# Attention context of a fused kernel: turned by VectorE in 32x32 blocks from a second load instead of by TensorE

## Chip, cores, metric

One NeuronCore of a Trainium2 chip. The metric is the device time of one execution in microseconds (us).

## What is computed

Two layers over 16 batches: a cross-attention with a residual, then a recurrent block on its result. The change touches the first layer, and in it the layer norm of the context and what follows from it:

```python
a = _layer_norm(audio_kv, ln_gamma, ln_beta)          # context (16, 375, 512)
Q = (hidden_states @ Wq.T)                            # tokens (16, 112, 512), 16 heads of 32
K = (a @ Wk.T); V = (a @ Wv.T)
scores = einsum('bhtd,bhsd->bhts', Q, K) * scale      # masked, softmax over the 375 keys
out = einsum('bhts,bhsd->bhtd', attn, V)
out = out.transpose(0, 2, 1, 3).reshape(B, Tt, D) @ Wo.T
return hidden_states + tanh(gate) * out
```

## The kernel before

The program is written engine by engine. Each engine has its own function with a fixed order of instructions, and the engines meet only through counted semaphores. Step `n` of the first layer works on three batches at once: it projects keys and values of batch `n` and forms its row-major scores (`scores`, 4 groups of 4 heads), it attends with batch `n-1` (`key_major_scores`, `weigh_values`), and it prepares the context of batch `n+1` (`ln_stats`, the normalised and turned copy, the query).

TensorE contracts over channels, so the context must lie with channels on partitions. Before, VectorE normalises the context with tokens on partitions (`ln_apply`, L430), TensorE turns it with 12 transposes a batch (`transpose_ctx`, L697) into three PSUM banks used in a ring, and ScalarE reads each turned bank twice, applying gamma and beta: once rounded (`aT_hi`, L572), once whole (`whole`, L576). GpSimd subtracts the two for the low part (`aT_lo`, L340). Keys and values are projected in three passes from the high and low parts (L703 to L705).

One region of PSUM, `score_bank`, holds both kinds of scores in turn, and this ties the engines together:

```python
pe.wait_ge(s_masked, count(later(m, 1), HEADS, g * HG))               # key_major_scores: VectorE has masked the scores in it
pe.wait_ge(s_shifted, count(later(b, -1), C * KT, (g + 1) * KT))      # scores: VectorE has read the key-major scores
```

`mask_scores` (L450) masks row-major scores and finds their extremes, `shift_scores` (L467) shifts key-major scores, `scale_attn` (L474) scales the attended values, and `project_out` (L789) waits for it.

All transfers of the first layer are issued by SyncE in one order (`sync`). The row statistics of a batch, turned by `turn_rows` (L782), are written to DRAM and read back spread over the partitions (`spread_rows`). The context mask for the key-major side is `key_mask8`, 125 partitions by 16 batches by 3 bytes (L296). The start loads context 0, the weights, both masks, context 1 and `wo`; VectorE needs the statistics of batch 1 within step 0.

## Time and profile before

| | us |
|---|---|
| median of 3 runs | 1405.7 (1401.32 to 1408.68) |
| profiled execution | 1402.65 |
| its span in the trace | 1400.8 |
| TensorE busy | 1331.3 (95%) |
| VectorE busy | 928.5 (66%) |
| ScalarE busy | 734.7 (52%) |
| GpSimd busy | 489.8 (35%) |

The first layer takes about the first 600 us, the second the rest. Busy time is a sum over a stage; whether an engine waits is read from the idle time before its instructions and from their order in time.

### The profile page before, as it was taken

To read this page: it belongs to the slowest core of one execution; us is meant where nothing else is said; L and a number is where in the kernel's file an instruction comes from. 1 tells how busy PE (TensorE), PEld (TensorE's weight loads), DVE (VectorE), ACT (ScalarE), POOL (GpSimd) and SP (SyncE) were. 2 spreads that over 40 slices of the span, in tenths; PEclk is the share of its full clock that TensorE was granted. 3 is DMA by queue.
4 is the path that set the end of the run, shared out by engine and by line. 5 is a ranking of instruction groups with operands and counts; after the bars stand their busy time and mean duration, and the time that the engine had idled before them with its cause. 6 is when DMAs were issued, how large, how long until landed. Compare 5 with 4: busy or idle time off the path is not lost.

```text
span 1400.8 us, 42823 instructions
## 1 busy us (share of the span) xinstructions
PE 1331.3 (95%) x17120; PEld 937.6 (67%) x17120; DVE 928.5 (66%) x2431; ACT 734.7 (52%) x1772; POOL 489.8 (35%) x550
## 2 busy tenths in 40 slices
PE   6999999999999999897899999999999999999977
PEld 5777777777777777666566666766676667666624
DVE  3555555555555555547677877787888888887862
ACT  4776677767667667632425453445345434444332
POOL 3222111222222222113346445543555345534540
PEclk9999999999999999988999999999999999999979
DMA  7333222222222223113000010001010110010000
GB/s 228 99 106 106 93 75 63 74 73 71 61 76 74 75 69 101 54 57 122 22 21 14 23 28 21 15 22 28 22 27 9 28 27 22 10 26 22 15 14 14
DMA packets 39529, 73.70 MB, mean 53 GB/s; under 512 B 17797, under 2 KB 20485, under 8 KB 37829
## 3 DMA queue, kind: packets, MB, share of 16 engines
q1 hardware_dynamic: 39365, 71.24, 17.2%
q8 instruction: 136, 2.23, 0.7%
q14 instruction: 28, 0.23, 0.1%
HBM read 60.24 MB, written 7.57 MB: 48 GB/s over the span
## 4 chain that ended last, share of the span: by engine, by line
PE 82%; DVE 8%; issue 6%; DMA 2%; ACT 1%; SPq 1%; POOL 0%; DVEq 0%; ACTq 0%; POOLq 0%
PE b_bank L1831 18%; PE b_bank L1837 12%; PE ring_bank L703 7%; PE ring_bank L704 6%; PE ring_bank L705 6%; PE av_bank L789 4%; PE b_bank L1945 4%; PE score_banks L762 4%; DVE probs L450 3%; PE b_bank L1982 3%; PE score_banks L749 3%; PE b_bank L1971 2%; PE b_bank L1885 2%; DVE probsT L467 2%; PE av_bank L775 2%
## 5 line engine op out<-in xcount | busy, mean ns | idle before, releaser
L1126 POOL TENSOR_TENSOR rst<-rp,st 128x448 f32<-128x448 f32 x192 | 209.7, 1115 | 55.9 <-DVE st L1349 53.9
L450 DVE CUSTOM_DVE_ANT_0 probs<-score_banks,unmask 112x375 f32<-112x375 f32 x256 | 124.8, 544 | 93.0 <-issue 93.0
L595 ACT ACTIVATE probs<-probs,least_inv 112x375 f32<-112x375 f32 x256 | 152.4, 606 | 32.5 <-DVE least_inv L450 32.5
L467 DVE SCALAR_TENSOR_TENSOR probsT<-score_banks,least_cols 125x448 f32<-125x448 f32 x192 | 107.9, 617 | 53.9 <-PE score_banks L762 51.7
L610 ACT ACTIVATE probsT<-probsT,key_mask 125x448 f32<-125x448 f32 x192 | 114.5, 661 | 47.4 <-DVE probsT L467 47.2
L1118 POOL TENSOR_TENSOR xm<-mixed,xa 128x448 f32<-128x448 f32 x80 | 88.0, 1102 | 145.3 <-DVE mixed L1278 140.0
L340 POOL TENSOR_TENSOR aT_lo<-whole,aT_hi 128x375 fp32r<-128x375 f32 x64 | 59.0, 921 | 152.3 <-ACT whole L576 150.2
L375 POOL TENSOR_TENSOR ctx_rstd<-ctx_var_eps,a_eps_exp 125x3 f32<-125x3 f32 x16 | 13.8, 865 | 272.6 <-DVE ctx_var_eps L423 272.6
L703 PE MATMUL ring_bank<-aT_hi,wk_lo 128*128 128x376 f32 x256 | 91.2, 356 | 0.2 <-issue 0.2
L1628 ACT COPY key<-b_bank 128x448 f32<-128x448 f32 x16 | 8.5, 533 | 148.4 <-PE b_bank L1831 148.4
L704 PE MATMUL ring_bank<-aT_lo,wk_hi 128*128 128x376 f32 x256 | 85.5, 334 | 0.0
L705 PE MATMUL ring_bank<-aT_hi,wk_hi 128*128 128x376 f32 x256 | 85.4, 334 | 0.0
L1278 DVE SCALAR_TENSOR_TENSOR mixed<-b_bank,vec_sb,sx 128x112 f32<-128x112 f32 x320 | 82.5, 323 | 1.8 <-PE b_bank L1885 1.8
L703 PE MATMUL ring_bank<-wv_hi,aT_lo 128*126 128x512 f32 x192 | 79.3, 413 | 0.4 <-DVE wv_lo L437 0.4
L1328 DVE TENSOR_TENSOR bv<-bv,ktil 128x392 f32<-128x392 f32 (+6 forms) x112 | 76.1, 679 | 3.9
L704 PE MATMUL ring_bank<-wv_lo,aT_hi 128*126 128x512 f32 x192 | 75.8, 395 | 0.0
L705 PE MATMUL ring_bank<-wv_hi,aT_hi 128*126 128x512 f32 x192 | 75.8, 395 | 0.0
L1945 PE MATMUL b_bank<-rst,b_collect 128*32 128x448 f32 x512 | 66.4, 556 | 3.5 <-POOL rst L1126 3.5
L1101 POOL TENSOR_TENSOR ln_rs<-ln_ve,neg_half 112x1 f32<-112x1 f32 x16 | 9.1, 571 | 171.5 <-DVE ln_ve L1245 171.5
L762 PEld LDWEIGHTS score_banks<-query,keyT 32*125 32x125 f32 x1536 | 47.7, 183 | 30.3 <-issue 19.6
L762 PE MATMUL score_banks<-query,keyT 32*125 32x112 f32 x1536 | 59.0, 282 | 9.2 <-DVE least_inv L450 6.9
L789 PE MATMUL av_bank<-wo_sb,attnT 128*112 128x512 f32 x128 | 61.3, 623 | 4.5 <-DVE attnT L474 3.8
(183 smaller groups left out, 3109.0 us busy)
## 6 DMA issues: line engine op xcount, KB each, us to landing
least_cols<-values_of_two_batches SPq DMA_DIRECT2D x32, 437.5 KB
ctx_tok<-in_ctx SPq DMA_DIRECT2D x16, 672.0 KB
xT_sb<-in_xT SPq DMA_DIRECT2D x16, 224.0 KB, 2.9
inv_cols<-values_of_two_batches SPq DMA_DIRECT2D x128, 28.0 KB, 3.9
x_tok<-in_x SPq DMA_DIRECT2D x16, 224.0 KB, 2.7
x_between_layers<-x_tok SPq DMA_DIRECT2D x16, 224.0 KB, 4.7
b_x<-x_between_layers SPq DMA_DIRECT2D x16, 224.0 KB, 3.0
x_post<-x_between_layers SPq DMA_DIRECT2D x16, 224.0 KB, 2.9
```

The costliest lines, as they stand in the source:

```text
L450: dve.tensor_tensor_reduce(out=probs[:, g % 2, i], in0=score_bank[0:T, i, 0:TC], in1=unmask[:, m[1]], scale=-SCALE, scalar=-LOWEST, op0=AL ...
L467: dve.scalar_tensor_tensor(out=probsT[:, g % 2, k].rearrange("p (i t) -> p i t", t=T), in0=score_bank[0:TK, :, k * T:(k + 1) * T], scalar= ...
L595: act.activation(probs[:, g % 2, i], probs[:, g % 2, i], ACT.Exp, scale=-1.0, bias=least_at(m, g, i), accum_out=sums[:, g, i:i + 1]).then_ ...
L703: pe.matmul(dst, ll, rh, start=start, stop=False)
L704: pe.matmul(dst, lh, rl, start=False, stop=False)
L705: return pe.matmul(dst, lh, rh, start=False, stop=stop)
L762: last = pe.matmul(score_bank[0:TK, i, k * T:(k + 1) * T], keyT[rows, m[1], g, k * TK:(k + 1) * TK], query[rows, m[1], g], start=True, sto ...
L789: last = pe.matmul(av_bank[0:T, :], attnT[:, c], wo[:, c], start=(c == 0), stop=(c == C - 1))
L1126: pool.tensor_tensor(by_chunk(rst[:, j % NPROD]), by_chunk(rp[:].rearrange("p c t -> p (c t)")), state_of(j), ALU.mult).then_inc(s_pprod, 1)
L1831: last = pe.matmul(dst[half, o * T:(o + 1) * T], w[:, c, o * P:(o + 1) * P][:, half], src[:, c], start=(c == 0), stop=(c == C - 1))
L1837: last = pe.matmul(dst[0:T, :], src[:, c], w[:, c], start=(c == 0), stop=(c == C - 1))
L1945: last = pe.matmul(out_bank[q * (P // QUAD):(q + 1) * (P // QUAD), 0:CT], collect[:, j], rst[:, j % NPROD], start=(r == 0), stop=(r == QUA ...
```

## The change

- The context is loaded twice. Once as before, for the statistics only, into a single buffer; once more as `ctx_quads`, where partition `q*32+r` holds channels `q*128` to `q*128+127` of token `k*32+r`. This takes 8 DMAs a batch (4 of 32x11 pieces of 512 bytes, 4 of 23).
- VectorE turns it with 4 transposes in 32x32 blocks (`turn_ctx`), then subtracts the mean and multiplies by the reciprocal deviation (`centre_ctx`, `scale_ctx`), each in two instructions of 128x750. Mean and deviation go through DRAM (`spread_stats`: write, wait, broadcast read), from SyncE's queue, for batch 0 from ScalarE's.
- ScalarE applies gamma and beta in SBUF (`affine_aT`, 4 a batch) and rounds (`copy_aT`, 4 a batch). The transposes on TensorE, `ctx_norm` and `whole` are gone.
- The query, before two units of two channel groups each, is now three units of one, one and two groups, placed where the transposes stood.
- Channels lie in a different order, so `wk` and `wv` are loaded in 4 DMAs each and gamma and beta in 8 more. Keys are now in plain token order, so the key mask is loaded as single bytes.
- Some semaphores are merged, with no instruction moved by it.

```diff
+RING = ["K0", "S1", "K1", "K2", "K3", "V0", "V1", "V2", "S0", "qa", "qb", "qc"]
+QUERY = {"qa": (0, 1), "qb": (1, 2), "qc": (2, 4)}
+    def load_quads(engine, b):
+        if at_least(b, 1):
+            engine.wait_ge(s_turned, count(later(b, -1), 1, 1))
...
+        for q in range(QUADS):
+            channels, rows = slice(q * P, (q + 1) * P), q * BLOCK
+            engine.dma_start(ctx_quads[rows:rows + BLOCK, 0:TB - 1],
+                             tokens[0:TC - TAIL, channels].rearrange("(k r) d -> r k d", r=BLOCK)).then_inc(s_quads, 16)
+            engine.dma_start(ctx_quads[rows:rows + TAIL, TB - 1], tokens[TC - TAIL:TC, channels]).then_inc(s_quads, 16)
+        def spread_stats(b):
+            sp.wait_ge(s_rstd, count(b, 1, 1))
+            sp.dma_start(stats_in_dram(b).rearrange("a (p k) -> p a k", k=KT), meanvar[:]).then_inc(s_stat_out, 16)
+            sp.wait_ge(s_stat_out, count(b, 16, 16))
+            sp.dma_start(stat_rows[:], stats_in_dram(b).rearrange("(o a) t -> o a t", o=1).broadcast_to([P, 2, TC])).then_inc(s_stat_in, 16)
-        sp.dma_start(key_mask8[:], A["mask"].rearrange("b (p k) -> p b k", p=TK),
+        sp.dma_start(key_mask8[:], A["mask"].rearrange("b (k p) -> p b k", p=TK),
+        def turn_ctx(b):
+            dve.wait_ge(s_quads, count(b, 32 * QUADS, 32 * QUADS))
             if at_least(b, 1):
+                dve.wait_ge(s_split, count(later(b, -1), C, C))
+            for c in range(C):
+                last = dve.transpose(ctxT[:, c].rearrange("p (k r) -> p k r", r=BLOCK), ctx_quads[:, :, c * BLOCK:(c + 1) * BLOCK])
+            last.then_inc(s_turned, 1)
+        def centre_ctx(b):
+            dve.wait_ge(s_stat_in, count(b, 16, 16))
+            dve.wait_ge(s_turned, count(b, 1, 1))
+            for h in range(2):
+                part = ctxT[:, 2 * h:2 * h + 2, 0:TC]
+                dve.tensor_tensor(part, part, stat_rows[:, 0:1].broadcast_to([P, 2, TC]), ALU.subtract).then_inc(s_cent, 1)
+        def affine_aT(b, c):
+            act.wait_ge(s_ctxn, count(b, 2, c // 2 + 1))
+            act.activation(ctxT[:, c, 0:TC], ctxT[:, c, 0:TC], ACT.Identity, scale=affine_ctx[:, 0, c:c + 1],
+                           bias=affine_ctx[:, 1, c:c + 1]).then_inc(s_whole, 1)
         def copy_aT(b, c):
...
+            if c == 0 and at_least(b, 1):
+                act.wait_ge(s_ring, unit_done(later(b, -1), "V2"))
+            act.wait_ge(s_whole, count(b, C, c + 1))
+            act.copy(aT_hi[:, c, 0:TC], ctxT[:, c, 0:TC]).then_inc(s_aT, 1)
```

TensorE, the end of a step with all parts (from the last row-major scores of group 2 to the output projection), before:

```order
L749 MATMUL score_banks<-keyT,query 112x375 x4
L782 MATMUL ring_bank<-ident_sb,least_inv 16x112
L697 MATMUL ring_bank<-ident_sb,ctx_norm 128x125 x9
L775 MATMUL av_bank<-probsT,value 32x112 x12
L762 MATMUL score_banks<-query,keyT 125x112 x12
L697 MATMUL ring_bank<-ident_sb,ctx_norm 128x125 x3
L737 MATMUL ring_bank<-xT_sb,wq_sb 64x112 x16
L749 MATMUL score_banks<-keyT,query 112x375 x4
L775 MATMUL av_bank<-probsT,value 32x112 x12
L737 MATMUL ring_bank<-xT_sb,wq_sb 64x112 x16
L789 MATMUL av_bank<-wo_sb,attnT 112x512 x4
```

And the same place now:

```order
L819 MATMUL score_banks<-keyT,query 112x375 x4
L852 MATMUL ring_bank<-ident_sb,least_inv 16x112
L807 MATMUL ring_bank<-xT_sb,wq_sb 64x112 x8
L845 MATMUL av_bank<-probsT,value 32x112 x12
L832 MATMUL score_banks<-query,keyT 125x112 x12
L807 MATMUL ring_bank<-xT_sb,wq_sb 64x112 x8
L819 MATMUL score_banks<-keyT,query 112x375 x4
L845 MATMUL av_bank<-probsT,value 32x112 x12
L807 MATMUL ring_bank<-xT_sb,wq_sb 64x112 x16
L859 MATMUL av_bank<-wo_sb,attnT 112x512 x4
```

The 12 transposes are gone, and one query group stands in the place of the first nine, one in the place of the last three and one group earlier. (A row of the order with `x8` is one query group; the trace has two records for each of its instructions, so there `x32` is two groups.)

SyncE at the start, from the first context 1 load to the first statistics, before:

```order
L248 DMA ctx_tok<-in_ctx 112x1536
L248 DMA ctx_tok<-in_ctx 13x1536
L253 DMA xT_sb<-in_xT 128x448
L295 DMA gate_sb<-in_gate 112x1
L296 DMA key_mask<-in_mask 125x16x3
L298 DMA wo_sb<-in_wo 128x2048
L253 DMA xT_sb<-in_xT 128x448 [waits ring_unit_done]
```

And now, from the last pieces of the second load of context 1:

```order
L261 DMA ctx_quads<-in_ctx 32x11x128
L263 DMA ctx_quads<-in_ctx 23x128
L286 DMA xT_sb<-in_xT 128x448
L337 DMA gate_sb<-in_gate 112x1
L338 DMA key_mask<-in_mask 125x48x1
L340 DMA wo_sb<-in_wo 128x2048
L286 DMA xT_sb<-in_xT 128x448 [waits ring_unit_done]
L279 DMA values_of_two_batches<-ctx_meanvar 125x2x3 [waits ctx_rstd_done]
L281 DMA ctx_stat_rows<-values_of_two_batches 128x2x375 [waits ctx_stats_written]
```

The key mask goes from 125x16 runs of 3 bytes to 125x48 of one, and the statistics of context 1 are issued behind it and behind `wo`.

VectorE in step 0 (batch 0 in its first projection, context 1 being prepared), now; before, `ln_stats` and `ln_apply` of context 1 stood around the second group of masks:

```order
L495 TENSOR_TENSOR wv_lo<-b_wv,wv_hi 128x512 [waits weights_rounded] x4
L484 TENSOR_TENSOR ctxT<-ctxT,ctx_stat_rows 128x2x375 [waits ctx_turned,ctx_stats_spread]
L484 TENSOR_TENSOR ctxT<-ctxT,ctx_stat_rows 128x2x375
L490 TENSOR_TENSOR ctxT<-ctxT,ctx_stat_rows 128x2x375 [waits ctx_centred] x2
L506 MEMSET score_seen 1x1 [waits score_done]
```

The last row opens the masks of group 1 of batch 0: they are now queued behind the wait for the spread statistics.

## Rows read from the trace of the kernel before

**Rows 1.** The page: busy us of each engine, share, instructions.

```profile
PE 1331.3 (95%) x17120; PEld 937.6 (67%) x17120; DVE 928.5 (66%) x2431; ACT 734.7 (52%) x1772; POOL 489.8 (35%) x550
```

**Rows 2.** Stretches: length, busy of PE, PEld, DVE, ACT, POOL, clock, DMA.

```profile
280.00:315.00 35.00, 34.63 (x387) 25.24 (x387) 18.55 (x63) 23.82 (x61) 7.57 (x10) 1.00 0.25 72
590.00:600.00 10.00, 7.07 (x35) 3.12 (x32) 4.13 (x16) 5.66 (x19) 0.00 (x0) 0.53 0.03 11
```

**Rows 3.** Groups of instructions from 100 to 525 us (12 steps).

```profile
L697 PE MATMUL ring_bank<-ident_sb,ctx_norm 125*128 125x125 f32 x144 | 20.0, 274 | 0.0
L576 ACT ACTIVATE whole<-ring_bank,vec_sb 128x375 f32<-128x375 f32 x48 | 32.1, 669 | 0.0
L430 DVE TENSOR_SCALAR ctx_norm<-ctx_tok,ctx_meanvar,ctx_rstd 125x512 f32<-125x512 f32 x36 | 17.9, 550 | 0.0
```

**Rows 4.** Timeline of PE at one step's end: start, length, what.

```profile
291.27 0.90 PE L749 MATMUL score_banks<-keyT,query 32*112 32x375 f32 x8
292.20 1.12 PE L697 MATMUL ring_bank<-ident_sb,ctx_norm 125*128 125x125 f32 x9
293.26 0.78 PE L775 MATMUL av_bank<-probsT,value 125*32 125x112 f32 x24
294.34 0.92 PE L762 MATMUL score_banks<-query,keyT 32*125 32x112 f32 x24 [0.30 <-DVE least_inv L450]
295.19 0.54 PE L697 MATMUL ring_bank<-ident_sb,ctx_norm 125*128 125x125 f32 x3
295.66 1.75 PE L737 MATMUL ring_bank<-xT_sb,wq_sb 128*64 128x112 f32 x32
297.34 0.90 PE L749 MATMUL score_banks<-keyT,query 32*112 32x375 f32 x8
300.71 3.69 PE L789 MATMUL av_bank<-wo_sb,attnT 128*112 128x512 f32 x8
```

**Rows 5.** Timeline of ACT (first row) and DVE, same step and next.

```profile
289.11 1.79 ACT L610 ACTIVATE probsT<-probsT,key_mask 125x448 f32<-125x448 f32 x3 [1.64 <-DVE probsT L467]
295.40 1.69 DVE L467 SCALAR_TENSOR_TENSOR probsT<-score_banks,least_cols 125x448 f32<-125x448 f32 x3 [1.11 <-PE score_banks L762]
300.27 0.38 DVE L474 TENSOR_TENSOR attnT<-av_bank,inv_cols 128x224 f32<-128x224 f32 x1
304.04 0.20 DVE L458 RECIPROCAL least_inv<-sums 112x8 f32<-112x8 f32 x1 [3.38 <-ACT probs L595]
310.65 0.54 DVE L450 CUSTOM_DVE_ANT_0 probs<-score_banks,unmask 112x375 f32<-112x375 f32 x1 [3.65 <-issue]
314.39 1.68 DVE L467 SCALAR_TENSOR_TENSOR probsT<-score_banks,least_cols 125x448 f32<-125x448 f32 x3 [1.78 <-PE score_banks L762]
```

**Rows 6.** Timeline of DVE and PE in the first 50 us.

```profile
27.69 2.49 DVE L437 TENSOR_TENSOR wv_lo<-b_wv,wv_hi 128x512 fp32r<-128x512 f32 x4
34.26 0.54 DVE L450 CUSTOM_DVE_ANT_0 probs<-score_banks,unmask 112x375 f32<-112x375 f32 x1 [1.74 <-issue]
39.80 0.90 PE L749 MATMUL score_banks<-keyT,query 32*112 32x375 f32 x8
48.52 0.92 PE L762 MATMUL score_banks<-query,keyT 32*125 32x112 f32 x24 [0.62 <-DVE least_inv L450]
```

**Rows 7.** Timeline of SyncE's issue of `wo` at the start: start, length.

```profile
11.14 14.92 SPq L298 DMA_DIRECT2D wo_sb<-in_wo  x1
```

**Rows 8.** DMA answer from 23 to 26.5 us: packets by size.

```profile
DMA packets 2095, 0.05 MB, mean 16 GB/s; under 512 B 2076, under 2 KB 2094, under 8 KB 2094
```

**Rows 9.** DMA answer, 294 to 300 us: packets, MB, share of 16 engines.

```profile
q1 hardware_dynamic: 450, 0.56, 28.8%
```

**Rows 10.** The page's issue list: KB each, us to landing.

```profile
xT_sb<-in_xT SPq DMA_DIRECT2D x16, 224.0 KB, 2.9
...
b_wo<-in_b_wo SPq DMA_DIRECT2D x1, 1024.0 KB, 5.0
...
values_of_two_batches<-least_inv_T SPq DMA_DIRECT2D x32, 7.0 KB, 1.3
```

More of the change, by code:

```diff
@@ L22 @@
 TE = TC + TC % 2
+BLOCK = 32
+QUADS = P // BLOCK
+TB = -(-TC // BLOCK)
+TAIL = TC - (TB - 1) * BLOCK
 C = D // P
@@ L306, in step @@
                 load_x(later(n, 2))
+            if normalise:
+                spread_stats(later(n, 1))
             if attend:
@@ L316, in step @@
                 load_ctx(later(n, 2))
+                load_quads(sp, later(n, 2))
             if project:
@@ L412, in ln_stats @@
         def ln_stats(b):
-            dve.wait_ge(s_ctx[b[1]], 32 * (b[0] + 1))
+            dve.wait_ge(s_ctx, count(b, 32, 32))
             for k in range(KT):
-                last = dve.bn_stats(stats[:, k], ctx_tok[:, b[1], k])
+                last = dve.bn_stats(stats[:, k], ctx_tok[:, k])
             last.then_inc(s_stats, 1)
             dve.wait_ge(s_stats, count(b, 2, 1))
+            if at_least(b, 1):
+                dve.wait_ge(s_stat_out, count(later(b, -1), 16, 16))
+                dve.wait_ge(s_ctxn, count(later(b, -1), 2, 2))
@@ L427, in ln_apply @@
+        def turn_ctx(b):
+            dve.wait_ge(s_quads, count(b, 32 * QUADS, 32 * QUADS))
             if at_least(b, 1):
-                dve.wait_ge(s_ring, unit_done(later(b, -2), "T3"))
-            for k in range(KT):
-                last = dve.tensor_scalar(ctx_norm[:, k], ctx_tok[:, b[1], k], meanvar[:, k, 0:1], rstd[:, k:k + 1],
-                                         ALU.subtract, ALU.mult)
-            last.then_inc(s_ctxn, 1)
+                dve.wait_ge(s_split, count(later(b, -1), C, C))
+            for c in range(C):
+                last = dve.transpose(ctxT[:, c].rearrange("p (k r) -> p k r", r=BLOCK), ctx_quads[:, :, c * BLOCK:(c + 1) * BLOCK])
+            last.then_inc(s_turned, 1)
@@ new lines, in centre_ctx, with scale_ctx @@
+        def centre_ctx(b):
[4 more added lines that the diff above has]
+                dve.tensor_tensor(part, part, stat_rows[:, 0:1].broadcast_to([P, 2, TC]), ALU.subtract).then_inc(s_cent, 1)
+        def scale_ctx(b):
+            for h in range(2):
+                dve.wait_ge(s_cent, count(b, 2, h + 1))
+                part = ctxT[:, 2 * h:2 * h + 2, 0:TC]
+                dve.tensor_tensor(part, part, stat_rows[:, 1:2].broadcast_to([P, 2, TC]), ALU.mult).then_inc(s_ctxn, 1)
@@ L512, in step @@
                 scale_attn(l, 1)
+            if normalise:
+                ln_stats(later(n, 1))
             if attend:
@@ L518, in step @@
                 shift_scores(m, 0)
+            if normalise:
+                turn_ctx(later(n, 1))
             if project:
                 mask_scores(n, 0, range(HG))
+            if normalise and not is_batch(n, 0):
+                centre_ctx(later(n, 1))
             if is_batch(n, 0):
@@ L525, in step @@
             if normalise:
-                ln_stats(later(n, 1))
+                if is_batch(n, 0):
+                    centre_ctx(later(n, 1))
+                scale_ctx(later(n, 1))
             if is_batch(n, B - 1):
@@ L654, in step @@
                 act.activation(tanh_gate[:], gate[:], ACT.Tanh).then_inc(s_gate, 1)
+            if normalise:
+                for c in range(C):
+                    affine_aT(p, c)
             if attend:
@@ L661, in step @@
             if normalise:
-                for c in range(3):
+                for c in range(C):
                     copy_aT(p, c)
+                copy_query(p, "a")
             if attend:
@@ L690, in free_unit @@
             return unit_bank(n, name)
-        def transpose_ctx(b, c):
-            dst = free_unit(later(b, -1), f"T{c}")
-            if c == 0:
-                pe.wait_ge(s_ctxn, count(b, 1, 1))
-            for k in range(KT):
-                last = pe.transpose(dst[:, k * TK:(k + 1) * TK], ctx_norm[:, k, c * P:(c + 1) * P], ident[0:TK, 0:TK])
-            last.then_inc(s_ring, 1)
         def by_parts(dst, left, right, start, stop):
@@ L851, in step @@
             if normalise:
-                for c in range(3):
-                    transpose_ctx(p, c)
+                project_query(p, "a")
             if attend:
```

158 lines of the change are left out of this document (84 added, 74 removed).

## Prediction

> **What bounds the kernel now.** I read the busy shares first: TensorE is at work for 95% of the span, no other engine for more than 66% [rows 1]. Then the stretches: in the first layer TensorE is busy 34.63 of 35 us [rows 2]. From these two alone, less work on TensorE is time won. The third view, the timeline of one step, says where that holds. The reader is to see that a step's end is a relay between TensorE and VectorE over one region of PSUM, and that TensorE is busy there because other work has been put between the legs [rows 4, 5].
>
> The three legs, for the step that ends at 300.71 us:
> - Row-major scores of group 2 start at 291.27, VectorE masks them, and the key-major scores may start at 294.34: 3.07 us, with TensorE idle for the last 0.30, ended by VectorE [rows 4]. VectorE sets this leg. The nine transposes lie in it.
> - Key-major scores start at 294.34, VectorE starts to shift them at 295.40 and takes 1.69, so to 297.09 [rows 5]. The next row-major scores start at 297.34 [rows 4]. From VectorE's end to TensorE's start I take 0.06 us, as between the attended values (300.27 + 0.38 = 300.65) and the output projection (300.71) [rows 4, 5]. The leg can be 2.81 us at best and is 3.00. Three transposes and two query groups (0.47 and 1.68 us, start to start) fill it.
> - Scores at 297.34 to the output projection at 300.71: 3.37 us, ended by VectorE's 300.65. VectorE sets it too.
>
> **Removed on TensorE.** 144 transposes take 20.0 us of busy time [rows 3], 0.139 us each, 1.67 a batch, 23.3 us in the 14 steps that attend and prepare (steps 1 to 14). If TensorE alone set the time, this would be the gain. But the new filler in the first leg is one query group, 1.68/2 = 0.84 us, for nine transposes that took 1.06 (292.20 to 293.26): TensorE comes 0.2 us earlier to a wait that already stood. In the second leg the filler falls from 2.15 to 0.84 us and TensorE reaches the wait on the shifts at 294.34 + 0.85 + 0.84 = 296.03, where VectorE ends at 297.09: about 1.1 us of new idle time, 0.19 us gained. The third keeps its two groups and its length. I take **0.2 us a step, 2.8 us in 14 steps**; the ends are 0 and the full 23.3.
>
> **Added to VectorE.** Its steady cost is nil if it fits the waits that exist. The statistics (2.5 us, from 315.99 before) go to the wait of 3.38 us before 304.04, the four transposes to that of 3.65 before 310.65, the two subtractions to that of 1.78 before 314.39; the two multiplications take the place of the statistics, which were longer [rows 5]. Subtraction and multiplication are 750 elements each: by `wv_lo`, 2.49/4 = 0.62 us for 512 [rows 6], I take 0.9 each, 1.8 a pair. A block transpose of 384 elements isn't in the trace. By the cheapest row of VectorE with its width, 0.550 us for 512 [rows 3], it would be about 0.4; from above, the gap allows 0.91 before masks are late. I take 0.5, nearer the row. The removed `ctx_norm` (three of 0.550) lay in slack as well. If the cover failed by x us before the masks of group 0, the step would lose at most x.
>
> The Trainium skill (Vector Engine (DVE) Microarchitecture Reference, "The reshape front-end and per-opcode configuration") has the transposing array sustain one element per cycle and lane. No row here shows it; it would leave my 0.5 as it is.
>
> **ScalarE** has eight activations a batch before and after. Four now stand before the exponentials of group 2. At 0.67 us each, overlapped (32.1/48) [rows 3], they are at most 2.7, against 1.64 us of wait there [rows 5], so the exponentials end at most 1.1 us later, 292.0, and the attended values that use them start at 293.26 [rows 4]. I take nothing.
>
> **DMA in a step.** The second load is about 1,500 packets of 512 bytes. 450 packets, some of 448 bytes and some of 1,792, took 28.8% of 16 queues for 6 us, 61 ns each [rows 9]. That is the upper end, 1500 x 61/16 = 5.7 us a batch; the lower is the rate of tiny packets, 2,076 in about 3.1 us [rows 8], so 2.2. I take 4.2. A step has room for it: the queues stand 75% idle [rows 2]. The statistics have a round trip of 1.3 us out and about 3 in (224 KB take 2.9) [rows 10] and some 8.5 us until they are used (304.0 to the end of the masks begun at 310.65). On SyncE the new issues stand before `spread_rows`, whose data come later still.
>
> **The start.** This is the largest term. Before, the masks of group 1 of batch 0 start at 34.26, row-major scores of group 2 at 39.80, step 1's first key-major scores at 48.52 [rows 6]. Now those masks are queued behind the subtraction for context 1, whose statistics SyncE issues behind key mask and `wo`. Step by step:
> - In the trace the key mask's packets run from about 23 us [rows 8] and SyncE, blocked on the issue of `wo`, comes free at 11.14 + 14.92 = 26.06 [rows 7]: 3.1 us for 2,000 runs of three bytes. 6,000 runs of one byte at that rate take 9.3.
> - Ahead of it now lie two second loads (2 x 4.2), a thousand four-byte elements of gamma and beta (1024 x 1.5 ns = 1.5) and batch 0's statistics (1): 10.9. Part of the first load uses queues that stood waiting; I take 9. The key mask runs from 32 to 41.3.
> - `wo` behind it: 5.0 us to landing [rows 10], to 46.3; statistics out with it; read back 3 us, 49.3.
> - Subtract and multiply, 3.6: masks of group 1 at 52.9.
> - From there a relay: masks 1.9, last exponential 1.1 later, copy of a value unit 0.5, tanh 0.3, four affines 2.2, another value copy 0.5, one query group 0.84, scores 0.9, latency 0.2, masks 1.9: 10.3. Key-major scores at 63.2 in place of 48.52: **14.7 us**.
> - ScalarE then still owes the exponentials of groups 2 and 3, about 1 us more than TensorE can hide: **1**.
> - TensorE stands mostly idle from about 46 to 60. In a stretch where it had little to do its granted clock fell to 0.53, near the lower of its two levels, 1.2 GHz of 2.4 [rows 2]. About 2 us of projections at half speed: **1**.
>
> The delay of the first key projection itself (statistics of batch 0 through DRAM, some 6 us) lies inside this and isn't added.
>
> The rule that speaks against this change is the Trainium skill's (DMA: Bandwidth & Descriptors, "Rules for kernel authors"): a strided last dimension becomes one descriptor per element. Before, the packet count of 2,076 agrees with one per three-byte run. By this rule the count is 6,000; were bytes what counts, 5.9 KB in both, the term would be 3.1 and the start 6.2 us better.
>
> **Sum.** 1402.65 (profiled execution) - 2.8 + 14.7 + 1 + 1 = 1416.6. That execution is 3 us under the median of its kernel, 1405.7, so on the median it would be near 1420. I state **1417**.
>
> **Rivals.**
> 1. *The start costs little* (22%). Ring order lets the statistics through early, or single bytes are moved as fast as triples. With 3.1 us for the key mask and 2.2 for each second load, masks come at 52.9 - 6.2 - 4 = 42.7; 10.2 less, so 1406. For it: no row has one-byte runs. Against: order in the queue.
> 2. *TensorE's work is the time* (10%), the faster side. If the relay could close up, as it would if VectorE's masks started earlier with scores shorter or if the idle of 0.30 were a passing one, steps gain 1.67 each: 23.3 - 16.7 = 6.6 us, 1396. It decides once more than 1.2 us a step is won. Against: all legs end on VectorE in the rows.
> 3. *A new wait in each step* (12%), slower still. ScalarE's affines hold the exponentials of group 2 and with them the attended values; if the four cost 1 us more than thought each step loses about 0.7: 1416.6 + 10 = 1427. For it: they are longer than the wait that they fill, by up to 1.1 us.
> 4. *The forecast* (56%): 1407 to 1430 by the ends of key mask (6 to 12 us) and second load (2.2 to 5.7).
>
> **Range and chances.** 0.5% of the time, 7 us, is what a measurement of this kernel can tell from no change. The forecast, less its low tail, and rival 3 are slower: 0.67. Rival 1 and that tail are within: 0.24. Rival 2: 0.09. The range runs from 1401 to 1431.
>
> **What would show it.** After: VectorE's first subtraction for context 1 at about 49 us, waiting for a DMA; the key-major scores of batch 0 at about 63; one step of a middle batch 0.2 us shorter, with about 1 us of TensorE's idle time before the scores of group 3, ended by VectorE's `probsT`; issue of `wo` ending near 41. Wrong if the middle steps shrink by more than 1 us, or grow, or if batch 1's statistics arrive before 42 us.

## The result, and the profile after

The changed kernel takes 1441.8 us (median of four runs, 1438.4 to 1444.8); the kernel before took 1403.5 beside it. The ratio is 1.027, with a 95% interval of 1.025 to 1.029. The forecast was 1417, with a range that ended at 1431. The direction was right and the size wrong by 25 us.

The profiled execution took 1438.4, with a span of 1436.6 us against 1400.8. Four marks on TensorE's timeline split the span: the first and the last output projection of layer 1, and the first and the last `xk` projection of layer 2. Of the kernel before:

```profile
81.63 1.11 PE L789 MATMUL av_bank<-wo_sb,attnT 128*112 128x512 f32 x2 [0.21 <-DVE attnT L474]
...
619.70 1.54 PE L789 MATMUL av_bank<-wo_sb,attnT 128*112 128x512 f32 x3
...
727.19 0.99 PE L1831 MATMUL b_bank<-xk,b_wfk 128*64 128x112 f32 x16
...
1386.22 0.99 PE L1831 MATMUL b_bank<-xk,b_wfk 128*64 128x112 f32 x16 [3.31 <-DVE xk L1420]
```

The same marks after the change:

```profile
111.22 1.11 PE L859 MATMUL av_bank<-wo_sb,attnT 128*112 128x512 f32 x2 [0.18 <-DVE attnT L532]
...
646.26 1.11 PE L859 MATMUL av_bank<-wo_sb,attnT 128*112 128x512 f32 x2
...
753.03 0.80 PE L1895 MATMUL b_bank<-xk,b_wfk 128*64 128x112 f32 x12
...
1422.03 0.80 PE L1895 MATMUL b_bank<-xk,b_wfk 128*64 128x112 f32 x12 [3.31 <-DVE xk L1484]
```

| stretch | before | after | difference | forecast |
|---|---|---|---|---|
| start to the first output projection | 81.6 | 111.2 | +29.6 | +16.7 |
| first to last output projection | 538.1 | 535.0 | -3.0 | -2.8 |
| from there to layer 2's first `xk` | 107.5 | 106.8 | -0.7 | 0 |
| first to last `xk` | 659.0 | 669.0 | +10.0 | 0 |
| to the end | 14.5 | 14.5 | 0 | 0 |

So the part between the output projections came out at the forecast's sum (not by its steps, as will be seen), the start is 12.9 us dearer than forecast, and 10.0 us appeared in a layer whose code the change doesn't touch.

**The steady step.** The page and one stretch, to be held against [rows 1, 2]:

```profile
PE 1312.3 (91%) x16928; PEld 920.0 (64%) x16928; DVE 996.2 (69%) x2511; ACT 725.4 (50%) x1788; POOL 494.0 (34%) x551
...
309.50:344.50 35.00, 33.42 (x376) 24.10 (x375) 22.61 (x68) 23.21 (x63) 7.77 (x10) 1.00 0.42 102
```

TensorE has 19 us less to do and is 33.42 of 35 us busy in place of 34.63; the DMA share rose from 0.25 to 0.42. The end of one step on TensorE and then VectorE, which answers to [rows 4, 5]:

```profile
320.42 0.90 PE L819 MATMUL score_banks<-keyT,query 32*112 32x375 f32 x8
321.25 0.26 PE L852 MATMUL ring_bank<-ident_sb,least_inv 112*16 112x112 f32 x1
321.45 0.99 PE L807 MATMUL ring_bank<-xT_sb,wq_sb 128*64 128x112 f32 x16
322.36 0.78 PE L845 MATMUL av_bank<-probsT,value 125*32 125x112 f32 x24
323.49 0.92 PE L832 MATMUL score_banks<-query,keyT 32*125 32x112 f32 x24 [0.34 <-DVE least_inv L508]
324.34 0.99 PE L807 MATMUL ring_bank<-xT_sb,wq_sb 128*64 128x112 f32 x16
326.38 0.90 PE L819 MATMUL score_banks<-keyT,query 32*112 32x375 f32 x8 [1.05 <-DVE probsT L525]
327.21 0.78 PE L845 MATMUL av_bank<-probsT,value 125*32 125x112 f32 x24
```

```profile
327.54 0.55 DVE L508 CUSTOM_DVE_ANT_0 probs<-score_banks,unmask 112x375 f32<-112x375 f32 x1
...
329.42 0.39 DVE L532 TENSOR_TENSOR attnT<-av_bank,inv_cols 128x224 f32<-128x224 f32 x1
329.72 1.87 DVE L458 BATCH_NORM_STATS2 ctx_stats<-ctx_tok 125x6 f32<-125x512 f32 x3
...
336.07 1.95 DVE L476 STREAM_TRANSPOSE ctxT<-ctx_quads 128x384 f32<-128x384 f32 x4
...
341.68 1.79 DVE L484 TENSOR_TENSOR ctxT<-ctxT,ctx_stat_rows 128x750 f32<-128x750 f32 x2
```

The reader is to see that the transposes are gone and that TensorE waits in their place: 1.05 us before the scores of group 3, ended by VectorE's `probsT`. The second leg takes 326.38 - 323.49 = 2.89 us (3.00 before), but the third, from 326.38 to the output projection at 329.86, takes 3.48 (3.37 before): behind the idle time VectorE's masks start 1.16 us after the scores do (327.54), where they started 1.06 after. Middle steps are 36.34 and 36.40 to 36.42 us in turn, 36.38 in the mean, where all were 36.41. The block transposes come to 1.95/4 = 0.49 us, a pair of subtractions to 1.79; 0.5 and 1.8 had been taken. None of them makes a step longer.

**The start.** VectorE's waits, and SyncE's issues, in the first 70 us:

```profile
14.35 1.96 DVE L476 STREAM_TRANSPOSE ctxT<-ctx_quads 128x384 f32<-128x384 f32 x4 [4.31 <-DMA ctx_quads<-in_ctx]
36.93 1.79 DVE L484 TENSOR_TENSOR ctxT<-ctxT,ctx_stat_rows 128x750 f32<-128x750 f32 x2 [20.63 <-DMA ctx_stat_rows<-values_of_two_batches]
...
63.25 1.79 DVE L484 TENSOR_TENSOR ctxT<-ctxT,ctx_stat_rows 128x750 f32<-128x750 f32 x2 [4.44 <-DMA ctx_stat_rows<-values_of_two_batches]
...
66.68 0.06 DVE L506 MEMSET score_seen<- 1x1 f32 x1
```

```profile
36.21 0.48 SPq L338 DMA_DIRECT2D key_mask<-in_mask  x1
36.73 14.86 SPq L340 DMA_DIRECT2D wo_sb<-in_wo  x1
...
52.11 0.33 SPq L279 DMA_DIRECT2D values_of_two_batches<-ctx_meanvar  x1
57.98 0.38 SPq L281 DMA_DIRECT2D ctx_stat_rows<-values_of_two_batches  x1
```

Masks of group 1 start at 66.7 (34.3 before, 52.9 forecast). ScalarE issued batch 0's statistics at 14.06, could read them back at 29.98, and VectorE had them at 36.93: a round trip of 22.9 us behind 3 MB of weights and batch 1's loads. TensorE had nothing to do meanwhile and came back at half its clock, which is the lower of its two levels, 1.2 GHz, and stayed there until 51.8 us (columns as in [rows 2]):

```profile
36.00:46.00 10.00, 0.00 (x0) 0.00 (x0) 8.56 (x16) 4.09 (x8) 3.44 (x4) 0.50 0.53 30
```

**Layer 2.** Four pauses of VectorE, each at the first instruction of its loop's body, 94 to 95 us apart, which is one turn (two steps). The first of them, and the page's line on VectorE's instruction packets:

```profile
894.80 0.57 DVE L1364 TENSOR_TENSOR gk<-key,wz 128x392 f32<-128x392 f32 x1 [4.27 <-issue]
...
q14 instruction: 49, 0.40, 0.1%
```

The kernel before has none, and 28 such packets. The four steps with a pause take 48.1 to 48.5 us, the ones between 46.0 (one 46.8).

### The profile page after: what moved, and what is told of

The parts are those of the page before. It is cut to its first block, busy times and chain, and to the rows that moved or that the text cites. A ratio compares the mean times of both kernels' runs of the same rounds, so it can differ in the third digit from the quotient of the medians.

```text
span 1436.6 us, 42814 instructions
## 1 busy us (share of the span) xinstructions
PE 1312.3 (91%) x16928; PEld 920.0 (64%) x16928; DVE 996.2 (69%) x2511; ACT 725.4 (50%) x1788; POOL 494.0 (34%) x551
## 3 DMA queue, kind: packets, MB, share of 16 engines
q10 hardware_dynamic: 2095, 1.16, 0.5%
## 4 chain that ended last, share of the span: by engine, by line
PE 66%; issue 12%; DVE 10%; POOL 5%; DMA 3%; SPq 2%; ACT 1%; ACTq 0%; DVEq 0%; POOLq 0%
PE b_bank L1895 14%; PE b_bank L1901 9%; PE ring_bank L772 6%; PE ring_bank L773 5%; PE ring_bank L774 5%; PE av_bank L859 4%; PE score_banks L832 4%; POOL rst L1191 3%; DVE probs L508 3%; PE score_banks L819 3%; PE b_bank L2010 3%; DVE probsT L525 3%; PE b_bank L2047 2%; PE b_bank L2036 2%; PE b_bank L1949 2%
## 5 line engine op out<-in xcount | busy, mean ns | idle before, releaser
L386 POOL TENSOR_TENSOR aT_lo<-ctxT,aT_hi 128x375 fp32r<-128x375 f32 x64 | 61.3, 991 | 362.5 <-ACT aT_hi L644 362.5
L807 PE MATMUL ring_bank<-xT_sb,wq_sb 128*64 128x112 f32 x1024 | 61.8, 271 | 21.1 <-DMA wq_sb<-in_wq 19.2
L819 PE MATMUL score_banks<-keyT,query 32*112 32x375 f32 x512 | 57.5, 518 | 17.0 <-DVE probsT L525 16.7
L772 PEld LDWEIGHTS ring_bank<-aT_hi,wk_lo 128*128 128x128 f32 x256 | 49.0, 191 | 34.8 <-issue 22.3
L807 PEld LDWEIGHTS ring_bank<-xT_sb,wq_sb 128*64 128x64 f32 x1024 | 51.9, 141 | 27.4 <-DMA wq_sb<-in_wq 19.2
```

The lines of the kernel that those rows point to most:

```text
L772: pe.matmul(dst, ll, rh, start=start, stop=False)
L807: last = pe.matmul(dst[half, i * T:(i + 1) * T], wq[:, c, m * P:(m + 1) * P][:, half], xT[:, b[1], c], start=(c == 0), stop=(c == C - 1))
```

## The experiments

All times of single kernels below come from one profiled execution. The changed kernel and five others with the same loads and the same order in the start (the six transposes, and the fills) had their first output projection between 111.2 and 116.7 us. In the same six the masks of group 1 started between 66.7 and 71.3, and the issue of `wo`, blocked behind the key mask, took 14.9 to 18.6 us. The changed kernel as profiled is the earliest of the six in all three, and its own four executions lie between 1438.4 and 1444.8. So differences of less than 5 us in one of these times, or of 6 in a total, decide nothing alone; what an engine waited for, and in what order things ended, does.

### Does the step stay a relay?

**Six transposes put back** into the second leg:

```diff
+            if name == "qb" and at_least(b, 1):
+                for _ in range(6):
+                    pe.transpose(dst[:, 0:P], ident[:], ident[:])
```

> The changed kernel with six transposes of the identity put back on TensorE in each step from batch 1 on, in front of the two matmul groups of the query unit of the second leg (their result is overwritten, so the output is the reference's). At 0.139 us each they are 0.83 us a step. Theory A (the step is a relay between TensorE and VectorE, and in the second leg TensorE stands idle for 1.05 us, ended by VectorE's probsT): the middle step stays at 36.38 us, the idle before the scores of group 3 falls from 1.05 to about 0.2, the total stays within 3 us of 1438. Theory B (TensorE's work sets the step): each step grows by 0.83 us, 14 steps by 12 us, to 1450.

Middle steps took 36.33 to 36.42 us, as without them. Its TensorE timeline at the same leg:

```profile
326.29 0.92 PE L835 MATMUL score_banks<-query,keyT 32*125 32x112 f32 x24 [0.34 <-DVE least_inv L508]
327.15 0.87 PE L806 MATMUL ring_bank<-ident_sb 128*128 128x128 f32 x6
327.95 0.99 PE L810 MATMUL ring_bank<-xT_sb,wq_sb 128*64 128x112 f32 x16
329.19 0.90 PE L822 MATMUL score_banks<-keyT,query 32*112 32x375 f32 x8 [0.25 <-DVE probsT L525]
```

0.8 us of work went in, the wait fell from 1.05 to 0.25, and the leg is 2.90 us. TensorE's work doesn't set the step. (Total 1441.7, within the start's spread.)

**Other work moved into the idle time.** The second leg gets two query groups, the third one, and the third leg also takes the first group of the next key projection, which stood at the head of the step:

```diff
-QUERY = {"qa": (0, 1), "qb": (1, 2), "qc": (2, 4)}
+QUERY = {"qa": (0, 1), "qb": (1, 3), "qc": (3, 4)}
...
-            if project:
+            if is_batch(n, 0):
                 project_key(n, 0)
...
                 project_query(p, "c")
+                project_key(p, 0)
```

> The changed kernel with work of TensorE moved into its new idle time: the middle query unit has two channel groups and the last one, and the first key projection of the next batch (2.05 us) stands at the end of the step before, not after the output projection. Theory A, the relay between TensorE and VectorE took the saving: with work put into the idle 1.05 us, a middle step falls from 36.38 us to 35.2 to 35.5, 12 to 16 us in 14 steps. Rival, another engine or wait sets the step: it stays above 36.2.

Middle steps fell to 35.22 to 35.30, 1.13 us less each; the total was 1427.1. The first output projection came at 117.2, at the late end of the spread above, so the total shows only part of the gain. So the removed transposes did leave something to win, but only once other work takes the place they left, inside the waits.

### What holds the start?

**Key mask in runs of three bytes** (tokens in another order than the values', so the mask is wrong for them):

```diff
-        A["mask"].rearrange("b (k p) -> p b k", p=TK)
+        A["mask"].rearrange("b (p k) -> p b k", p=TK)
```

> The changed kernel with the key mask loaded in runs of three bytes again (2,000 runs in place of 6,000; the tokens of the mask are then in the old order, which only permutes its values). Theory A, each run of the last dimension costs the same whatever its bytes: the issue of wo, 14.9 us long from 36.7 us on, ends about 7 us earlier, the masks of group 1 of batch 0 (66.7 us) come 6 to 7 us earlier and the total falls by as much. Rival, the key mask's place in the queue and not its size counts: under 1.5 us. Nothing changes before 36 us or in the steps of either layer by either.

The issue of `wo` ended at 41.2 in place of 51.6, 10.4 us earlier (7 expected), but masks of group 1 came only 4.9 us earlier, at 61.7, and the total was 1435.4. SyncE, free at 41.7, then waited 8.4 us until batch 1's statistics were there to be written. SyncE's wait and GpSimd's instruction that ended it:

```profile
SPq L279 <- POOL ctx_meanvar L418: 8.4, 1, 8.4
...
49.18 0.88 POOL L418 TENSOR_TENSOR ctx_meanvar<-ctx_var_eps,a_eps_exp 125x3 f32<-125x3 f32 x1
```

GpSimd forms batch 1's reciprocal deviation behind the split of batch 0 (`aT_lo`, 42.2 to 46.1) and a mask, and the split waits for batch 0's late statistics. In the changed kernel the same instruction ended at 50.4, only 1.2 us before SyncE was free of `wo`. So a second chain is nearly as long as the queue: batch 0's round trip, ScalarE's copies, GpSimd's split, batch 1's deviation. VectorE's own work behind batch 0's key projection was as late: it waited just 0.41 us for batch 1's statistics.

**Batch 0's statistics protected.** SyncE issues nothing behind `wk` until they are back:

```diff
         load_turned("wk")
+        sp.wait_ge(s_stat_in, 16)
```

> The changed kernel, with SyncE holding back mask, wv, context 1 and all later loads until the statistics of batch 0 are back in SBUF. Theory A, these statistics (written at 14.1 us, seen at 30.0, back at 36.9) wait behind the weights' and contexts' packets in the DMA queues: the round trip falls from 23 us to 6 to 10, the first key projection comes at 30 to 34 us in place of 46.6, and the total falls by little, 0 to 5 us, since the masks of group 1 are then bound by the later loads. Rival, the tiny runs themselves (12 bytes to DRAM) are slow: the round trip stays above 18 us.

Their round trip fell from 22.9 to 11.6 us and the first key copy came 11 us earlier. The later loads were issued later, the first piece of context 1's second load by 13 us, and the issue of `wo` ended at 55.3 in place of 51.6: VectorE waited 15.7 us for batch 1's statistics, masks of group 1 at 70.5, total 1439.1, both within the spread of the changed kernel.

**The same, with key mask and `wo` behind batch 1's statistics:**

```diff
-        sp.dma_start(key_mask8[:], ...)
-        sp.dma_start(wo[:], A["wo"]).then_inc(s_w["wo"], 16)
...
                 spread_stats(later(n, 1))
+            if is_batch(n, 0):
+                sp.dma_start(key_mask8[:], ...)
+                sp.dma_start(wo[:], A["wo"]).then_inc(s_w["wo"], 16)
```

> The changed kernel with two edits of SyncE's order at the start: it waits for batch 0's statistics to come back before it issues anything behind the load of wk, and it issues key mask and wo only behind the spread of batch 1's statistics. Theory A (each batch's statistics wait behind loads that were queued ahead of them, and the masks of group 1 wait for them): batch 0's statistics are back at 26 us as in the run with the hold alone, those of batch 1 are subtracted without the 15.7 us wait that stood there, masks of group 1 at 52 to 58 in place of 66.7, the first output projection at 97 to 103 in place of 111.2, the total at 1425 to 1431. Theory B (key projection 0 and the work of TensorE and ScalarE behind it set the start once the first statistics are late at all, whatever the queues hold): masks of group 1 come down, but the first output projection stays above 108, the total within 3 us of 1438. The wait for wo itself (5 us to land) can take some of A's gain.

Masks of group 1 came at 57.3, 9.4 us earlier, and all of it was lost again. The first output projection stood at 111.9, since VectorE then waited for the least scores that also pass through DRAM:

```profile
79.96 1.69 DVE L527 SCALAR_TENSOR_TENSOR probsT<-score_banks,least_cols 125x448 f32<-125x448 f32 x3 [8.13 <-DMA least_cols<-values_of_two_batches]
```

SyncE issued those behind 13.3 us of blocked `wo` issue and batch 2's loads, at 69.06. The numbers are theory B's (above 108, total 1438.6), but both theories had a part right: the queue was the cause each time, but freeing one trip made the next one late.

**One more order:** with the hold and with `wo` behind batch 1's statistics, the key mask goes to ScalarE's queue, and batch 0's first least scores ahead of batch 2's loads.

```diff
+        act.dma_start(key_mask8[:], ...)      # ScalarE, behind its own two
...
+                sp.dma_start(wo[:], A["wo"]).then_inc(s_w["wo"], 16)
+                spread_rows(n, 0)
```

> The changed kernel with the start's queue in another order: SyncE issues nothing behind wk until batch 0's statistics are back, ScalarE's queue takes the key mask right behind those statistics, and SyncE issues wo behind batch 1's statistics and the spread of batch 0's first least scores ahead of batch 2's two loads. In the run with the statistics first, the masks of group 1 came 9 us earlier and the key-major scores then waited 8.1 us for those least scores, which SyncE could issue only behind wo and the loads of batch 2. Theory A (each DRAM round trip of the start pays for what SyncE has queued ahead of it): that wait falls below 3 us, the first output projection comes at 97 to 103 in place of 111.9, the total at 1423 to 1429. Theory B (what remains is the chain of engines behind the late first key projection): the first output projection stays above 108 and the total above 1433. The one risk to A is that the key mask's 6,000 elements now share the queues with batch 1's loads.

Theory A fell: 1446.2, first output projection at 121.6. No wait for the least scores was left, but the risk named was the result. Beside the key mask's elements batch 1's loads crawled (one `ctx_quads` issue blocked SyncE for 6.6 us), `ctx_tok` of batch 1 was waited for until 45.4, 13.8 us, and its statistics came back at 60.5; later VectorE waited 7.1 us for batch 2's.

**No round trip for batch 0** (statistics replaced by two rows of the context, so batch 0's values are not the reference's):

```diff
         load_quads(act, (0, 0))
+        act.dma_start(stat_rows[:], A["ctx"][0, 0:2, 0:TC]...broadcast_to([P, 2, TC])).then_inc(s_stat_in, 16)
...
-        act.wait_ge(s_rstd, 1)
-        act.dma_start(stats_in_dram((0, 0))..., meanvar[:]).then_inc(s_stat_out, 16)
-        act.wait_ge(s_stat_out, 16)
-        act.dma_start(stat_rows[:], stats_in_dram((0, 0))...).then_inc(s_stat_in, 16)
```

> The changed kernel without the round trip of batch 0's statistics: two rows of the context, 375 elements each, are spread over the partitions by a load issued right behind the context's second load, so VectorE subtracts and multiplies without waiting for DRAM (values of batch 0 are not the reference's, the work is the same). The first key projection waited for that trip from 16.3 us to 36.9. Theory A (the prediction's: the delay of the first key projection is hidden in the later wait for batch 1's statistics): key projection 0 comes some 20 us earlier, at 26 to 30, but the masks of group 1 stay within 3 us of 66.7, the first output projection within 3 us of 111.2. Theory B (it isn't hidden, since what follows is a chain that starts with that projection and the queue's work adds to it): the first output projection comes 10 to 20 us earlier, 91 to 101, the total at 1418 to 1428.

Theory A, the prediction's own step. The first key projection came at 33.9, 12.8 us earlier (not the 16 to 20 expected, since ScalarE then waited for `wk` until 24.4), and the first output projection at 111.23 against 111.22. But the masks of group 1 still started at 65.9, since VectorE now waited for batch 1 instead. And from there to the key-major scores it took 12.4 us (10.6 in the changed kernel), with TensorE's granted clock at its lower level from 60.6 to 77.7 us. The timeline of VectorE:

```profile
17.43 1.79 DVE L487 TENSOR_TENSOR ctxT<-ctxT,ctx_stat_rows 128x750 f32<-128x750 f32 x2 [1.58 <-DMA ctx_stat_rows<-in_ctx]
...
62.42 1.79 DVE L487 TENSOR_TENSOR ctxT<-ctxT,ctx_stat_rows 128x750 f32<-128x750 f32 x2 [16.17 <-DMA ctx_stat_rows<-values_of_two_batches]
```

**The same, with the key mask in runs of three:**

> The same kernel, with the key mask loaded in 2,000 runs of three bytes (tokens in another order than the values'; the mask values are wrong for it) in place of 6,000 of one. Alone, that freed the queue 10 us earlier and won 4 us at the first output projection, because the chain behind the late first key projection bound then. With that chain early as well, theory A for the queue (batch 1's statistics wait for the key mask and wo) says that now nearly all of the 10 us show: first output projection 8 to 11 us before that of the run above, the total 7 to 11 us below it. If only 0 to 4 us show, something else than the queue holds batch 1, and the start's cost stays open in that part.

Masks of group 1 at 56.8, 9.0 us earlier than in the run above, first output projection at 101.1, 10.1 us earlier; total 1421.9, 12 below. Both lie far outside the spread. Alone each edit had won 0 and 4 us at the first output projection, no more than the spread; together 10. Two chains end at the masks of group 1: batch 0's round trip with all that waits for it (key projection, split, batch 1's deviation), and the queue up to batch 1's statistics. The second alone ends at 65.9 (the run without the first), the first at about 61.7 (the run with the shorter queue). With the first gone and the second 9 us shorter they start at 56.8, still ended by the statistics (7.05 us of wait).

### What holds layer 2?

> The kernel before, with 41 extra one-element memsets on VectorE at its very start (0.06 us each, under an idle stretch of 6.4 us), by which its later instructions stand as far from the program's beginning as those of the changed kernel. Theory A, the four gaps of 4.1 to 4.5 us before the first gk of a loop turn in the second layer come from where the loop's instructions lie: the same four gaps appear and the total rises by 8 to 10 us. Rival, they come from what the change left in the DMA queues or in timing: no gap, total within 3 us of the kernel before.

The edit is 41 one-element fills of an unused tile ahead of VectorE's first statistics, in the kernel *before*. It took 1408.8 us, at the top of what that kernel took without them (1398.9 to 1409.0). No pause of 4 us appeared, but four of 1.3 to 1.6 did, at the same instruction, and the packets rose from 28 to 48. Layer 2 took 659.9 us between its marks (659.0 without fills), so neither theory's numbers came out:

```profile
868.77 0.57 DVE L1303 TENSOR_TENSOR gk<-key,wz 128x392 f32<-128x392 f32 x1 [1.53 <-issue]
...
q14 instruction: 48, 0.39, 0.1%
```

Then 23 such fills in the changed kernel:

> The changed kernel with 23 one-element fills of an unused tile on VectorE ahead of its first statistics, so that every later instruction of VectorE stands 23 places further on. It asks about the four gaps of 4.1 to 4.5 us at the first instruction of VectorE's loop in layer 2. Theory A (they depend on where the loop's body lies in VectorE's instruction stream): gaps change, to none or to another size, and layer 2 comes back by up to 9 us, 1429 to 1433. Theory B (something in the changed kernel other than place, such as the state in which layer 1 leaves a queue): four gaps of about 4.3 us remain, 1437 to 1441. The kernel before with 41 fills had none, which speaks for B or for a place that 41 fills don't reach.

The pauses were gone and layer 2 took 659.4 us between its marks (669.0 without fills):

```profile
q14 instruction: 30, 0.25, 0.1%
```

The total, 1436.2, kept little of these 10 us since this run's first output projection was 5.5 us later. Of these, 2.1 stood at the masks of group 1 already, behind an issue of `wo` of 16.3 us in place of 14.9; the rest I did not settle.

For the rule behind it, 256, 150 and 128 fills in the changed kernel:

> The changed kernel with 256 fills on VectorE ahead of its first statistics, in place of 23. The four gaps at the head of VectorE's loop in layer 2 were there with 0 fills, gone with 23, and the kernel before had none, but four of 1.3 to 1.6 us with 41 fills. Theory A (what counts is where the loop's body lies against blocks of 256 instructions, of which two are held): with 256 fills it lies as with none, so four gaps of 4.0 to 4.5 us are back and the count of VectorE's instruction packets is near 49. Theory B (any shift away from the place of the changed kernel helps, or the place counts by another period): no gaps, packets near 30. The fills themselves cost some 15 us ahead of the first statistics, so the total says nothing here; layer 2's first to last load-free product, 669 us against 659, does. The Trainium skill (Advanced Engine Details and Errata, "ISA Cache") gives 16 KB lines of 256 instructions and two lines; by it A.

> The changed kernel with 150 fills on VectorE. Theory A (blocks of 256 instructions, two held): the bad places are those where the loop's body reaches into a third block. The kernel before was good with 0 fills and bad with 41, and the changed one, 41 places on, bad with 0 and good with 23: so the bad stretch is at least 1 and at most 63 places long and ends before 64. 150 fills are outside it: no gaps, packets near 30, layer 2 at 659 us. Theory B (another period, such as 64 or 128 places): 150 is 22 past 128 and past two times 64, and reads as 22 fills, good as well; it would tell nothing alone, but 256 fills, bad by A, are bad by B too. Only a gap here speaks against both.

> The changed kernel with 128 fills. With 0 and with 256 fills the four gaps are there, with 23 and with 150 they aren't: that is a period of 256 places, but one of 128 fits as well (150 is 22 past 128), and the fills of the run with 256 showed pauses 128 fills apart. Theory A (blocks of 256): 128 fills lie outside the bad stretch, no gaps, some 30 instruction packets. Theory B (blocks of 128): 128 fills read as none, four gaps of 4.0 to 4.5 us, some 50 packets.

| fills | 0 | 23 | 128 | 150 | 256 |
|---|---|---|---|---|---|
| pauses, us | 4.1 to 4.5 | none | 3.7 to 4.6 | none | 4.2 to 4.8 |
| VectorE's instruction packets | 49 | 30 | 51 | 30 | 51 |
| layer 2, first to last `xk` | 669.0 | 659.4 | 668.1 | 660.8 | 669.0 |
| first output projection | 111.2 | 116.7 | 116.3 | 114.7 | 112.9 |
| total | 1438.4 | 1436.2 | 1437.2 | 1431.1 | 1439.7 |

The pauses are back at 128 fills, so the period isn't 256 places; 128 fits, and by the fills alone a divisor of it would too. The packets speak for 128: 21 of them moved 0.17 MB from 850 to 1200 us, 8 KB each, and that is 128 instructions at the 64 bytes which the Trainium skill gives (Vector Engine (DVE) Microarchitecture Reference, "Instruction fetch and dispatch (NX sequencer)"). The Trainium skill's rule (Advanced Engine Details and Errata, "ISA Cache": 32 KB in two lines of 256) agrees in kind, but not in its line: by it the bad stretch, which is over at 23 fills, should come back at 256 and not at 128.

### All that helped, together

The moved work with the two edits of the statistics' order:

> The last kernel with the moved work of the run before it (the query unit of the second leg has two groups in place of one, that of the first leg and the third one fewer, and the first group of the next key projection stands in the third leg). By theory A the edits add up: 14 steps of 1.13 us less (15.8), and 7 to 13 less at the start; with 9 us of VectorE's gaps in layer 2 still in: 1409 to 1416, so 0.5 to 1% slower than the kernel before. If the relay and the start share what they save, as the run of the moved work alone suggested (first output projection 6 us later, 11 us of the 15.8 kept), it comes to 1418 to 1424.

1423.1 us over four runs, ratio 1.013 (1.0105 to 1.0155), as the second of the two sums had it. With 23 fills and ScalarE's queue for the key mask:

> The last kernel with the moved work of TensorE (1.13 us less a step, 15.8 in 14) and with the 23 fills on VectorE that took away the four gaps of layer 2 (9 to 10 us). From 1438: 15.8 less, of which the run with the moved work alone kept 11, 9 less in layer 2, and 9 to 14 less at the start by theory A: 1400 to 1409, so from 0.3% under to 0.4% over the kernel before. By theory B for the start: 1412 to 1418. If the gaps come back, because moved instructions put VectorE's loop elsewhere, 9 more.

1423.5, ratio 1.016 (1.014 to 1.017), above both forecasts. Middle steps at 35.2 to 35.3 and a layer 2 without pauses, but a first output projection at 124.0, by the start's order that had fallen alone. No kernel here beat the one before. The moved work with fills and the changed kernel's own start wasn't run; by its parts I estimate 1427 - 10 = 1417, with the start's spread on it.

## Why the prediction was wrong in size

**What bounds the kernel: right. "0.2 us a step": right in the sum, wrong in the step.** The relay, the place of the idle time, what ends it and its length are the forecast's. But the second leg gained 0.11 us in place of 0.19, the third, which was to keep its length, lost 0.11, and a middle step gained 0.03. The 3.0 us come mostly from the last two of the 15 intervals (38.83 to 38.21, and 24.98 to 23.36), which the forecast didn't treat apart. That the sum agrees is chance: the last interval alone took 21.8 to 27.1 us in the other kernels here. The rival that TensorE's work is the time fell to the six transposes put back. The rival of a new wait in each step fell too: the affines hold nothing up.

**VectorE's costs: right**, within 0.02 us each. The statistics' round trip in a middle step, put at 1.3 + 3 us, took 6.5 to 7.3, still inside its room of 8.5.

**"6,000 runs of one byte at that rate take 9.3": too low.** The key mask's packets lie between 37.9 and 52.1 us, 14.2 us; the forecast had 32 to 41.3. From 38 to 48 us:

```profile
DMA packets 5130, 0.04 MB, mean 4 GB/s; under 512 B 5081, under 2 KB 5130, under 8 KB 5130
```

These took about 2 ns each over 16 queues, the last 840 some 4 us more. In runs of three bytes the 2,000 packets took 4.7 us (37.1 to 41.8). So it is 2.4 ns a packet for one byte as for three, where 1.55 was taken, and 4,000 more packets cost 9.9 us of `wo`'s issue (14.86 against 4.95), where the sum had 6.2. By bytes it would be nothing; the rule of one descriptor per element (the Trainium skill, DMA: Bandwidth & Descriptors, "Rules for kernel authors") holds here, and packets set the price.

**"Ahead of it now lie ...: 10.9 ... I take 9": the step that failed most.** The key mask's first packet came at 23.1 us before and at 37.9 after, 14.8 us later. The queues' time until then, before (0 to 23.09 us) and after (0 to 37.85):

```profile
q1 hardware_dynamic: 1486, 5.89, 83.2%
...
q1 hardware_dynamic: 5090, 6.65, 77.1%
q10 hardware_dynamic: 2095, 1.16, 17.4%
```

That is 19.2 and 35.8 us of all 16 queues, 16.6 more. Sorted by packet size, the two second loads (512 bytes) take 8.4 of them, as forecast; gamma and beta 1.2; batch 0's statistics 1.8. Another 4.1 had no term at all: `wk` and `wv` are now loaded in 1,024 packets of 2,048 bytes where they were 256 of 8,192. The rest is 1. Of the 16.6, 1.8 were hidden in queues that had stood waiting, as forecast (1.9). SyncE was blocked on issues of batch 1's second load nearly all the time from 16.7 to 34.5 us.

**"`wo` behind it ...; read back 3 us": too low.** SyncE's issue of `wo` ended at 51.6, not at "near 41". From there to the statistics' use at 63.25 it took 11.7 us, where 5 + 3 were counted; the read back alone took 5.3. Together: 10.3 us at `wo`, 3.7 behind it, 0.2 less for VectorE's work, 13.8 us, and masks at 66.7 where 52.9 was forecast. With batch 0's trip taken away, so that only this chain is left, the same numbers are 50.7, 11.7 and 65.9, so it is the queue that sets them.

**"The delay of the first key projection ... some 6 us ... isn't added": right that it is hidden, by luck.** Its size was wrong by a factor of four (26.3 us, from 20.3 to 46.6). It is hidden only because the queue was longer still, by 1.2 us at the point where batch 1's statistics can be written; had the queue been as forecast, this chain would have set masks at about 61.7, 9 us later than forecast.

**From the masks to the key-major scores: right.** 66.68 to 77.30, 10.6 us against 10.3. For the clock and ScalarE's exponentials 2 us were added behind them; the delay grew from 28.8 us there to 29.6 at the first output projection, 0.8.

**Layer 2: not in the forecast at all.** VectorE's loop there was refetched in every turn, which 23 fills on VectorE took away. By the order's count 41 more instructions stand ahead of it; that the loop then no longer fits what the engine holds is argued below, not shown. 1416.6 + 12.9 + 10.0 - 0.9 (the table's second and third rows against the forecast) gives 1438.6, against 1438.4 measured.

**The rivals.** "The start costs little" is out. The range's upper end, 1431, held neither the queue's error nor a cost in code that the change doesn't touch.

## What to carry to other kernels

- Work taken off the busiest engine is won only where that engine isn't waiting in a relay. Look for the wait that ends each leg, and put other work in the idle time that the edit leaves: 0.03 us a step became 1.16.
- A round trip through DRAM costs what is queued ahead of it. In a middle step it took 6.5 to 7.3 us and nothing waited for it; behind weights it was 23 us. Freeing one such trip made the next one late (15.7, then 8.1 us). So count all of them in the start together, in packets and not in bytes, and every load that the change cuts into smaller pieces with them: weights in four parts cost 4.1 us that no term had.
- Before two versions are compared, look for pauses "<-issue" at the first instruction of a loop and at the instruction packets. A few dozen instructions more or less elsewhere on an engine (here 23) can make 10 us of difference in a loop that nobody touched.

## What the runs showed of the hardware

VectorE's loop is refetched in every turn at some places: 5 packets of 8 KB a turn, with a pause of 1.3 to 4.8 us at the loop's head, and none at others. By the fills and the packets' size the places come back every 128 instructions. That loops touching four such blocks fit and loops touching five don't would explain the counts; the loop's length in instructions as fetched isn't in the trace, so this is argued, not shown. Why the pause was 1.5 us in the kernel before and 4.3 in the changed one is open.

A small write to DRAM was not protected by going through ScalarE's own queue: from issue to the read behind it 15.9 us while SyncE's loads filled the 16 queues, 7.9 with nothing issued behind `wk`.

The same loads in the same order don't take the same time: the 6,000 one-byte packets of the key mask took 14.2 to 18.0 us in six kernels that differ only in other engines' work. What makes the difference is open.
